# Another order of the second attention and the MLP's first half in a one-core FP32 decoder block on Trainium2

## The reference, cut to what matters

```
x = x + tanh(g_xattn[0]) * attention(layernorm(x), ctx)          # 16 heads, softmax
x = x + tanh(g_ffn[0])   * moe(layernorm(x))                     # 8 experts, top 2
x = x + tanh(g_xattn[1]) * autocorr(layernorm(x), ctx)           # below
x = x + tanh(g_ffn[1])   * fp4_mlp(layernorm(x))                 # below

autocorr: Q, K, V = projections, 16 heads of 8
  corr = irfft(rfft(Q) * conj(rfft(K))), mean over the head width
  w, idx = top_k(corr, 4); w = softmax(w)
  out = sum_k w_k * V rolled by idx_k;  return out @ Wo + bo
fp4_mlp: q(.) rounds blocks of 16 values to FP4 and scales back
  h = silu(q(x) @ q(Wg)^T) * (q(x) @ q(Wu)^T);  return q(h) @ q(Wd)^T
```

## Time and profile before

| what | us |
|---|---|
| median of three runs | 312.07 |
| lowest, highest | 311.04, 312.18 |
| the profiled execution's own time | 312.27 |
| its span, first to last instruction | 310.5 |
| TensorE busy | 260.1 (84%) |
| VectorE busy | 205.5 (66%) |
| ScalarE busy | 163.6 (53%) |
| GpSimd busy | 114.7 (37%) |

### The profile page before, as it was taken

One profiled execution on the slowest core, in us unless ns is written; L12 is line 12 of the kernel. 1 busy time (PEld: TensorE's weight loads), 2 busy tenths in 40 slices (PEclk: granted clock), 3 DMA queues, 4 the chain that ended last, 5 costly groups with the idle time before them and its releaser, 6 DMA issues.

```text
span 310.5 us, 6172 instructions
## 1 busy us (share of the span) xinstructions
PE 260.1 (84%) x2126; PEld 199.1 (64%) x2126; DVE 205.5 (66%) x556; ACT 163.6 (53%) x381; POOL 114.7 (37%) x163
## 2 busy tenths in 40 slices
PE   2999889999898988999999994987892857598675
PEld 1565257666667935999999993666661424467474
DVE  3499988888986355342322337663989499999951
ACT  1169365666584578775566553762327352434321
POOL 3174549993202103229952202300554303231230
PEclk9999999999999999999999999699997588979957
DMA  7994000000000208676777710000000000001011
GB/s 246 357 387 196 0 3 2 2 2 0 3 2 2 74 2 364 262 303 276 292 291 305 291 70 3 1 0 2 0 0 1 0 2 0 0 17 34 19 34 35
DMA packets 11871, 30.13 MB, mean 97 GB/s; under 512 B 961, under 2 KB 5057, under 8 KB 11713
## 3 DMA queue, kind: packets, MB, share of 16 engines
q1 hardware_dynamic: 11840, 29.75, 25.2%
HBM read 9.75 MB, written 1.05 MB: 35 GB/s over the span
## 4 chain that ended last, share of the span: by engine, by line
PE 53%; DVE 30%; ACT 7%; issue 5%; DMA 3%; POOL 1%; SPq 0%; DVEq 0%
PE ps L1223 10%; PE ps L1214 9%; PE ps L1104 5%; DVE s_region L276 4%; PE ps L1078 4%; PE ps L1091 4%; DVE s_small L225 3%; DVE s_region L680 3%; PE ps L1401 2%; DVE s_small L967 2%; DVE s_region L272 2%; PE ps L1114 2%; PE ps L1283 2%; DMA s_region<-s_wall 2%; PE ps L1379 2%
## 5 line engine op out<-in xcount | busy, mean ns | idle before, releaser
L542 ACT ACTIVATE s_region<-ps,s_region 128x128 f32<-128x128 f32 x144 | 40.8, 371 | 20.5 <-PE ps L1214 20.4
L834 DVE SCALAR_TENSOR_TENSOR s_ctxT<-ps,s_region,s_ctxT 128x64 f32 x72 | 18.1, 281 | 45.7 <-PE ps L1223 45.4
L1214 PE MATMUL ps<-s_region 128*128 128x128 f32 x288 | 37.9, 276 | 0.8 <-DVE s_ctxT L810 0.5
L1223 PE MATMUL ps<-s_region 128*128 128x128 f32 x288 | 38.0, 276 | 0.5 <-ACT s_region L542 0.5
L1214 PEld LDWEIGHTS ps<-s_region 128*128 128x128 f32 x288 | 34.9, 192 | 1.8 <-DVE s_ctxT L810 1.3
L1223 PEld LDWEIGHTS ps<-s_region 128*128 128x128 f32 x288 | 35.0, 192 | 0.9 <-ACT s_region L542 0.7
L1379 PE MATMUL ps<-s_region 128*128 128x352 f32 x64 | 25.9, 558 | 11.3 <-DVE s_region L957 6.1
L283 POOL TENSOR_TENSOR s_region<-s_region,s_small 128x704 f32<-128x704 f32 (+2 forms) x13 | 17.5, 1343 | 47.6 <-DVE s_region L276 47.6
L248 POOL TENSOR_TENSOR s_small<-s_small,s_par 128x4 f32<-128x4 f32 (+3 forms) x14 | 15.5, 1108 | 47.1 <-DVE s_small L231 47.1
L380 POOL COPY s_region<-s_xt 128x64 f32 x72 | 14.9, 240 | 40.2 <-PE ps L1214 21.9
L490 ACT COPY s_region<-ps 128x512 f32<-128x512 f32 x32 | 17.2, 589 | 18.2 <-PE ps L1091 18.2
(11 more groups left out here) (205 smaller groups left out, 507.0 us busy)
## 6 DMA issues: line engine op xcount, KB each, us to landing
s_region<-s_wall SPq DMA_DIRECT2D x36, 514.0 KB, 3.2
s_wall<-wall SPq DMA_DIRECT2D x8, 514.0 KB, 9.2
s_par<-par SPq DMA_DIRECT2D x1, 1316.0 KB, 11.1
s_ctxT<-ctxT SPq DMA_DIRECT2D x2, 512.0 KB, 6.0
s_x<-x SPq DMA_DIRECT2D x2, 512.0 KB, 7.4
out<-s_x SPq DMA_DIRECT2D x8, 128.0 KB, 1.8
s_region<-ffn SPq DMA_DIRECT2D x1, 560.0 KB, 3.6
s_par<-par SPq DMA_DIRECT2D x1, 460.0 KB, 3.8
```

The source lines that it names most:

```text
L542: ins = act.activation(hg[j % 3][:, c, :], ps[:, j % 3, RPT * S * c:RPT * S * (c + 1)], ACT.Gelu, bias=wbuf[j % 6][:, FF + FC * D + c:FF + ...
L834: dve.scalar_tensor_tensor(row, ps[:, 4 + j % 2, S * k:S * k + S], w, row, ALU.mult, ALU.add).then_inc(m["acc_done"], 1)
L1214: ins = mm(ps[:, j % 3, RPT * S * c:RPT * S * (c + 1)], w[:, P * c:P * c + P], xg[j % 4], start=True, stop=True)
L1223: ins = mm(ps[:, 4 + j % 2, 0:RPT * S], w[:, FF + D * c:FF + D * c + D], hg[j % 3][:, c, :], start=(c == 0), stop=(c == FC - 1))
```

## The change

It is one of order, with two PSUM banks renamed; the computation stays as it is, and no instruction is added or dropped apart from waits. ScalarE normalises groups 0 and 1 of the second attention and VectorE groups 2 and 3. The table loads for exp and silu move to earlier places of ScalarE's queue. TensorE's list of the entry is reordered. VectorE runs `roll_values(0)` to `(3)` one behind the other, defers the additions of the bias, and puts `x_scale(0)` between rolls 5 and 6. `x_round(1)` stands inside the loop, behind `pair_step(0)`, and the steps of groups 2 and 3 move one place. `gate_up(0)` waits for the rolls, `gate_up(1)` also for the last copy of `y1_turned`, and the wait for `x3_done` goes to `turn_h(0)`.

```diff
@@ gpsimd @@
-            for q in range(PAIRS):
-                if q == 6:
-                    powers(pool, 0, 4)
...
+            for q in range(4):
+                values_added(q)
+            powers(pool, 0, 4)
+            values_added(4)
+            values_added(5)
             powers(pool, 4, 8)
+            values_added(6)
+            values_added(7)
+            x_unscale(0)
             powers(pool, 8, 12)
-            x_unscale(0)
             powers(pool, 12, 16)
             x_unscale(1)
...
-                if g < G4 and q % 2 == 1:
-                    x_unscale(g)
+                if q in (2, 4):
+                    x_unscale(q // 2 + 1)
@@ scalar @@
                 if j == 6:
                     act.wait_ge(m["ld_ffn"], 16)
                     act.activation(wm, wnat, ACT.Abs).then_inc(m["wabs_ready"], 1)
+            preload(ACT.Exp)
 
             for g in range(3):
                 act.wait_ge(m["wq_tr"], g + 1)
...
             normalise(act, 0, 4, m["xn_c"], 7)
+            x_turned(0)
             normalise(act, 4, 8, m["xn_c"], 8)
-            x_turned(0)
-            normalise(act, 8, 12, m["xn_c"], 9)
+            q_turned(0)
             x_turned(1)
-            q_turned(0)
-            normalise(act, 12, 16, m["xn_c"], 10)
             x_turned(2)
             q_turned(1)
+            q_turned(2)
             x_turned(3)
-            q_turned(2)
+            heads_turned(0)
             q_turned(3)
-            preload(ACT.Exp)
-            heads_turned(0)
             exp_lead(0)
             heads_turned(1)
             turn_gx(0)
             exp_lead(1)
+            preload(ACT.Silu)
             turn_gx(1)
...
+            normalise(act, 0, 4, m["xn_d"], 11)
             y1_turned(2)
-            normalise(act, 0, 4, m["xn_d"], 11)
-            y1_turned(3)
             normalise(act, 4, 8, m["xn_d"], 12)
             x_magnitude(0)
-            preload(ACT.Silu)
+            y1_turned(3)
+            turned_x(0)
             normalise(act, 8, 12, m["xn_d"], 13)
-            turned_x(0)
+            silu(0)
             x_magnitude(1)
-            silu(0)
             normalise(act, 12, 16, m["xn_d"], 14)
-            turned_x(1)
...
-                if g < G4 and q % 2 == 0:
-                    x_magnitude(g)
+                if q in (1, 3):
+                    x_magnitude((q + 3) // 2)
...
-                if q in (2, 4):
+                if q in (0, 2, 4):
                     turned_x(q // 2 + 1)
@@ vector @@
+            normalise(dve, 8, 12, m["xn_c_late"], 9)
+            products(0)
+            normalise(dve, 12, 16, m["xn_c_late"], 10)
+            products(1)
             dve.tensor_scalar(bo1g, pc("bo1"), tg[:, 2:3], None, ALU.mult)
-            for g in range(G4):
-                products(g)
+            products(2)
+            products(3)
             best_lags(0)
             best_lags(1)
             for q in range(4):
                 roll_values(q)
-                bias_added(q)
-            roll_values(4)
...
+            bias_added(0)
+            bias_added(1)
+            out_and_stats(0)
+            roll_values(4)
             roll_values(5)
-            out_and_stats(0)
+            out_and_stats(1)
+            x_scale(0)
             roll_values(6)
             roll_values(7)
-            out_and_stats(1)
+            x_round(0)
+            bias_added(2)
             out_and_stats(2)
-            x_scale(0)
-            attention_out(3)
-            x_round(0)
-            x_stats(3)
+            bias_added(3)
+            out_and_stats(3)
             x_scale(1)
-            x_round(1)
             for q in range(PAIRS + 3):
-                g = q // 2 + 2
                 pair_step(q)
-                if g < G4:
-                    (x_scale if q % 2 == 0 else x_round)(g)
+                if q in (0, 2, 4):
+                    x_round(q // 2 + 1)
+                if q in (1, 3):
+                    x_scale((q + 3) // 2)
@@ tensor @@
             to_frequency(0)
+            queries(0)
             to_frequency(1)
-            queries(0)
             to_frequency(2)
             queries(1)
+            sum_heads(0)
+            queries(2)
             to_frequency(3)
-            queries(2)
-            sum_heads(0)
+            sum_heads(1)
             queries(3)
-            sum_heads(1)
             correlate(0)
...
             spectrum(4)
+            spectrum(5)
             out_tokens(0)
-            spectrum(5)
             out_product(1)
+            out_tokens(1)
             spectrum(6)
-            out_tokens(1)
             spectrum(7)
-            for g in range(2, G4):
-                out_product(g)
-                out_tokens(g)
+            out_product(2)
+            out_tokens(2)
+            out_product(3)
+            out_tokens(3)
...
                 if t >= 2:
                     pe.wait_ge(m["hh_done"], t // 2)
                 else:
-                    pe.wait_ge(m["x3_done"], G4)
+                    pe.wait_ge(m["of_done"], 2 * PAIRS)
+                    if t == 1:
+                        pe.wait_ge(m["y1_ready"], G4)
...
                 pe.wait_ge(m["hq_done"], q + 1)
                 if q:
                     pe.wait_ge(m["ht_used"], q)
+                else:
+                    pe.wait_ge(m["x3_done"], G4)
...
             gate_up(0)
             gate_up(1)
-            turn_x(1)
...
-                if q in (2, 4):
+                if q in (0, 2, 4):
                     turn_x(q // 2 + 1)
```

More of the change, by code:

```diff
@@ L403, in _, with values_added @@
                 powers(pool, 4 * g, 4 * g + 4)
-            for q in range(PAIRS):
-                if q == 6:
-                    powers(pool, 0, 4)
+            def values_added(q):
                 pool.wait_ge(m["of_done"], 2 * q + 2)
@@ L414, in x_unscale @@
                 fp4_unscale(pool, qd[g % 2], xsc[g % 2], 4 * D // BLK, qv[g % 2]).then_inc(m["xq_done"], 1)
+            for q in range(4):
[3 more added lines that the diff above has]
+            values_added(5)
             powers(pool, 4, 8)
+            values_added(6)
+            values_added(7)
+            x_unscale(0)
             powers(pool, 8, 12)
-            x_unscale(0)
             powers(pool, 12, 16)
             x_unscale(1)
-            for q in range(PAIRS + 1):
-                g = q // 2 + 2
[L423 to L428, removed]
-                if g < G4 and q % 2 == 1:
-                    x_unscale(g)
+            for q in range(1, PAIRS + 1):
+                u = (q - 1) % 2
+                pool.wait_ge(m["hd_done"], q)
+                if q >= 3:
+                    pool.wait_ge(m["ht_done"], q - 2)
+                fp4_unscale(pool, hd[u], hsc[(q - 1) % 3], 2 * NH, hq[u].rearrange("p a n -> p (a n)")).then_inc(m["hq_done"], 1)
+                if q in (2, 4):
+                    x_unscale(q // 2 + 1)
         @block.scalar
@@ L585, in y1_turned @@
                 act.wait_ge(m["y1_done"], g + 1)
-                act.copy(y1.rearrange("p a b -> p (a b)"), ps[:, 2, :]).then_inc(m["y1_ready"], 1)
+                act.copy(y1.rearrange("p a b -> p (a b)"), ps[:, 4, :]).then_inc(m["y1_ready"], 1)
             normalise(act, 0, 4, m["xn_c"], 7)
+            x_turned(0)
             normalise(act, 4, 8, m["xn_c"], 8)
-            x_turned(0)
-            normalise(act, 8, 12, m["xn_c"], 9)
+            q_turned(0)
             x_turned(1)
-            q_turned(0)
-            normalise(act, 12, 16, m["xn_c"], 10)
             x_turned(2)
             q_turned(1)
+            q_turned(2)
             x_turned(3)
-            q_turned(2)
+            heads_turned(0)
             q_turned(3)
-            preload(ACT.Exp)
-            heads_turned(0)
             exp_lead(0)
@@ L909, in bias_added @@
                 dve.wait_ge(m["bo_scaled"], 1)
-                dve.wait_ge(m["xn_c"], 4 * g + 4)
+                dve.wait_ge(m["xn_c_late" if g >= 2 else "xn_c"], 4 * (g % 2) + 4)
                 dve.tensor_tensor(x[:, 4 * g:4 * g + 4, :], x[:, 4 * g:4 * g + 4, :],
@@ L931, in attention_out @@
                 dve.wait_ge(m["o_done"], g + 1)
-                dve.scalar_tensor_tensor(group(x, g), ps[:, 3, :], tg[:, 2:3], group(x, g), ALU.mult, ALU.add).then_inc(m["x3_done"], 1)
+                dve.scalar_tensor_tensor(group(x, g), ps[:, 5, :], tg[:, 2:3], group(x, g), ALU.mult, ALU.add).then_inc(m["x3_done"], 1)
             def x_stats(g):
@@ L1257, in to_frequency @@
             def to_frequency(g):
-                pe.wait_ge(m["xn_c"], 4 * g + 4)
+                pe.wait_ge(m["xn_c_late" if g >= 2 else "xn_c"], 4 * (g % 2) + 4)
                 if g >= 2:
@@ L1335, in out_product @@
                 for k in range(4):
-                    ins = mm(ps[:, 2, P * k:P * k + P], of1[:, 4 * g + k, :], pc("wo1"), start=True, stop=True)
+                    ins = mm(ps[:, 4, P * k:P * k + P], of1[:, 4 * g + k, :], pc("wo1"), start=True, stop=True)
                 ins.then_inc(m["y1_done"], 1)
```

(2 more changed lines are left out.)

4 lines of the change are left out of this document (1 added, 3 removed).

## The result

| | runs | median us | lowest, highest |
|---|---|---|---|
| before, beside it | 4 | 311.81 | 311.04, 312.18 |
| changed | 4 | 316.25 | 314.59, 317.52 |

The ratio is 1.0116 with a 95% interval of 1.0068 to 1.0163. Applied to the 312.07 us of the prediction this is 315.7 us. That is 1.9 us above the number, above the forecast's own range (312.9 to 315.0) and 0.1 us inside the upper end of the whole range, 315.8; the median itself, 316.25, lies 0.45 us above that end. The kernel got slower, as forecast. Medians here are of all runs, while ratios leave out those that lie far above the others of the same kernel, as five of the nine in e11, the kernel of before, do (316.76 us and more) and the run of which e2 has its profile (320.14 us). The profiled execution took 317.52 us, with a span of 315.7.

A forecast was written before the change was run, and what follows sets the result against it. The end was taken as set by pair_step(0)'s start and VectorE's remaining work. 312.27 us plus 0.2 (entry), 0.25 (pair_step(0)) and 1.35 (x_round(1)) gave 314.1, stated as 313.8; own range 312.9 to 315.0, whole range 309.9 to 315.8.

The forecast's parts named there:

- What bounds the kernel: Kernel's end: set by when pair_step(0) can start and VectorE's work left then; VectorE has no gap worth naming in the loop.
- Entry: Entry of the second attention, up to the second lags: between -0.5 and +1.2 us, taken as +0.2.
- The table loads: ScalarE's exp and silu loads, moved into its waits: costed at nothing, 1.28 us each with the activation 1.29 us after.
- VectorE's normalise: Second attention's entry: 340 ns a tile inside VectorE's wait for the first queries, free; about a microsecond's hold-up with powers(3) covered.
- Rolls: Rolls 0 to 3 without bias additions between: attention_out(0) at 226.75 instead of 227.44, VectorE then about 1.9 us behind.
- MLP entry: From attention_out(0) to pair_step(0): roll 7 comes late, TensorE's clock falls, pair_step(0) at 248.75, +0.25 us.
- Rival 1: Ahead of the loop, TensorE keeps its clock and gate_up(1) ends at 244.0: total 310.6 or 310.0 us, chance 0.22.
- x_round(1): Moved behind pair_step(0), from VectorE's idle time into the part that has none: +1.35 us.
- In the loop: Steps of groups 2 and 3 move by one pair: costed at nothing; silu(2) up to 0.8 us late at a low clock.
- Sum: Whole kernel: 312.27 + 0.2 + 0.25 + 1.35 = 314.1 us, given as 313.8.
- signs of being wrong: In the changed profile: pair_step(0) before 247, full clock over gate_up(0), or idle time of VectorE inside the loop.
- signs of being right: Include queries(0) at 196.9, TensorE idle before out_product(3), clock 0.50 over gate_up(0), about 3 us idle before pair_step(0).

The follow-up runs named there:

- e11: The kernel of before run once more, unaltered, for a second profile: ratio 1.0015.
- e2: The changed kernel with the loop's order put back as it was before: ratio 1.0005, median 312.15 us.
- e4: The kernel of before with only the new entry of the second attention: ratio 0.9983.
- e8: The kernel of before, order untouched, with unread matmuls at five places where TensorE idles: ratio 0.9838, median 307.08 us.
- e9: The kernel of before with the new entry, the unread matmuls of e8 and one more ahead of queries(0): ratio 0.9813, median 306.10 us.
- e7: The kernel of e2 (changed kernel, loop's order as before) with unread matmuls at five places: ratio 0.9937, median 309.90 us.
- e1: The changed kernel with only x_round(1) put back ahead of the loop, x_magnitude(1) ahead of silu(0): ratio 1.0049, median 313.84 us.
- e6: The changed kernel with six unread matmuls ahead of down(5) in the tail: ratio 1.0102, median 315.16 us.
- e0: The changed kernel run again with nothing altered: ratio 1.0141, median 315.63 us.
- e10: The changed kernel run a third time, unaltered, for its profile: ratio 1.0074, median 314.61 us.
- e3: The kernel of before with only the loop's new order: ratio 1.0107, median 314.94 us.
- e5: The changed kernel with three unread matmuls ahead of each of turn_x(2) and turn_x(3): ratio 1.0018, median 312.19 us.

## Why the prediction was right, and which steps failed

**What bounds the kernel: right for before, half right for after.** With the loop's order of before, e11, e2, e4, e8 and e9 all have 48.05 to 48.08 us in the loop; only e7 has 48.89, with two waits. Lines 276 and 272 are helpers that also work ahead of the loop, but 90% of their part in the chain of the earlier trace rows is in it. What I missed: I treated the loop as VectorE's in any order. In the changed one it is VectorE's work plus waits for TensorE.

**Entry: wrong in sign and size.** I took +0.2, between -0.5 and +1.2; it was -0.85, outside my bounds. The order of events was as told, down to the gap ahead of `queries(0)`. In after, the last lags began 27.24 us behind `moe_out(0)` against 27.59 in my schedule, before any surcharge for the clock: the hand-overs around `correlate` were shorter than I counted. The clock did come back later (in the stretch at 204 us, thus 12 us behind `moe_out(0)`, where it had been 11), but `sum_heads(1)` ended 19.3 us behind `moe_out(0)`, as in my schedule: the 0.7 us that I had added for the clock did not show. One profile does not settle the size: with the same instructions the new entry took 26.67 us in e1 and 28.07 in e6. e8 and e9 give the term at a mean clock of 1.00 in both: 26.99 against 25.44, so the reorder itself is worth some 1.5 us there.

**The table loads: free, as costed.** They ran at 188.14 and 220.51 in the changed kernel:

```profile
188.14 1.28 ACT L439 ACT_TABLE_LOAD   x1
189.43 0.20 ACT L439 ACTIVATE s_small<-s_par 128x1 f32<-128x1 f32 x1
...
220.51 1.28 ACT L439 ACT_TABLE_LOAD   x1
221.80 0.20 ACT L439 ACTIVATE s_small<-s_par 128x1 f32<-128x1 f32 x1
```

The activation follows 1.29 us after the load's start, as in the earlier trace rows. The Trainium skill's 2.66 us for a switch (ScalarE: Activation LUTs, section What ACT_TABLE_LOAD costs) do not show here either.

**VectorE's normalise: free, as costed.** It took 1.11 us for four tiles both times, once beside GpSimd's `powers(3)`; the hold-up of about a microsecond did not come.

**Rolls: right order, a little too dear.** I expected `attention_out(0)` 10.0 us behind the second lags and over 2 us of idle time ahead of it; it was 9.64 and 1.55 us.

**MLP entry: right mechanism.** I expected 22.0 us from `attention_out(0)` to `pair_step(0)` with the clock low over `gate_up`; it was 21.65 with 4.41 us for `gate_up`. Rival 1 came true for this part in e0 and e10: 19.85 us with `gate_up` at the full clock. It made these little or no faster from `moe_out(0)` on (123.30 and 122.83 against 123.80 us), since the loop waited 1.3 and 0.9 us more there. All ahead of `pair_step(0)` I had at +0.45; it was -1.30.

**x_round(1): 1.35 predicted; it is in the loop's work, but not simply paid.** The loop's 3.33 us are 1.34 for it, 1.81 of waiting, and 0.18 that is left over and not traced. Yet e1 shows that putting it back alone returns only 0.58 us, because it covers a wait for silu(1).

**In the loop: this step failed.** "I cost this at nothing" was wrong: 1.81 us in the first profile, 1.19 + 1.96 in e0, 0.76 + 1.96 in e10, 1.13 + 2.82 in e3. I had named the mechanism, a low clock over the transposed group's `gate_up`, with a price of up to 0.8 us for silu(2), and looked at the wrong group: group 1 was in time in the first profile (in e3 and e10 silu(2) was late too), and group 3 was late in all. `gate_up(12)` and `(13)` took 4.17 to 5.06 us in all six profiles that have group 3's steps in their new places and no matmuls added there. The chain of group 3 is `x_round(3)` at 282.70 to 284.1, `x_unscale`, `turn_x(3)` from 285.31, its copy, `gate_up` from 286.64. At the full clock it ends within 0.3 us of its need (e5); it had no slack left (the two pairs ahead that I counted were 5.7 us, from the rounding's end at 284.1 to VectorE's need at 289.8), and TensorE's idle time ahead of it lowered the clock. With the order of before the rounding comes one pair earlier, TensorE goes from `turn_h` to `turn_x(3)` without a gap, and `gate_up(12)` and `(13)` take 2.63 us, which is in time by 0.03 us. The low clock is in that loop too (0.92 on the mean in both kernels), but in that profile it fell on `gate_up` of groups 1 and 2 (4.05 and 3.88 us), where it was hidden. These rows stood in the trace before the prediction: they would have told that group 3 had no room for a later start or a low clock.

**Sum.** +1.8 predicted and +1.96 measured from `moe_out(0)` on, but with the entry 1.75 us too dear and the loop 1.98 too cheap. The sum was near because two errors cancelled, which is luck. And the time measured is further off than that: the medians lie more above before than these 1.96 us, by what lies ahead of the change.

**The signs.** My own list of signs of being wrong had idle time of VectorE inside the loop, and it came in the first profile (1.81 us). e0 and e10 show the full clock over `gate_up(0)` as well. Of the signs of being right, the gap ahead of `queries(0)`, the idle time of TensorE before `out_product(3)` (1.95 us) and the low clock over `gate_up(0)` came in the first profile; the wait before `pair_step(0)` was 2.20 us instead of about 3.

**What is not settled.** The medians lie 2.5 to 4.4 us above those of before, the profiles from `moe_out(0)` on only 1.0 to 2.0. In two of three profiles of the changed kernel the rest is low clock ahead of the change, 3.2 and 3.5 us. Four of ten profiles with the new entry have `moe_out(0)` after 191 us, and none of the four without it (before, e11, e3, e8). The instructions ahead are the same in all but for the exp load, which runs some 3.8 us ahead of `moe_out(0)`, long after the two low stretches. Before has longer runs too, of which no profile was kept. Whether the program makes this more frequent or it fell so by chance is open.

## What to carry to other kernels

A step may be moved only as far as its whole chain has slack, and the slack has to be counted at the low clock, because being late makes TensorE idle and the idling makes what follows late once more. Read for every moved group the slack between its last product and its use, not only for the first. Judge a reorder by its stretches in the profile: here a gain of 1.3 us and a loss of 3.3 stood in one change, and with the loss undone (e2) the time was that of before.

## What had not been expected of the hardware

The same program differs by over 3 us with the places at which TensorE's clock falls, in stretches far from any change. Unread matmuls in gaps of 1.6 to 5 us raise the clock for what comes behind: five places of them made the kernel 1.6% faster with no change of order (e8), and together with the new entry 1.9% (e9). Here they worked only where the gap did not come back one step later: in e6 the tail stayed as it was, 13.79 us, until a second gap was filled too, which gave 11.66 us in e8 and e9. A kernel with none of them in its tail has one of 11.6 us at times too (e1, e3, e5), so one profile does not price it.
